# Six of sixteen probability blocks per pass turned by DMA transposes between two GpSimd copies, in an attention block on one core

## What is computed

```
q = split_heads(layernorm(x) @ Wq + bq);  k = split_heads(ctx @ Wk + bk);  v = split_heads(ctx @ Wv + bv)
scores = einsum('bhqd,bhkd->bhqk', q, k) / sqrt(32)
attn = softmax(scores, axis=-1)
out = einsum('bhqk,bhkd->bhqd', attn, v)  ->  @ Wo + bo
```

## Time and profile before

| what | value |
|---|---|
| median of 3 runs | 515.05 us (514.48 to 515.17) |
| the profiled execution | 515.1 us, its span 513.3 us, granted TensorE clock 0.998 |
| TensorE (PE) busy | 495.2 us, 96% |
| PE's weight loads | 378.2 us, 74% |
| VectorE (DVE) busy | 307.7 us, 60% |
| ScalarE (ACT) busy | 266.2 us, 52% |
| GpSimd (POOL) busy | 42.2 us, 8% |
| chain that ended last | PE 83%, ACT 7%, DVE 5%, issue 4% |

### The profile page before, as it was taken

How to read it: one execution, slowest core, us unless ns; L and a number is a source line. 1 busy time by engine, 2 the same in 40 slices (tenths; PEclk the granted TensorE clock), 3 DMA queues, 4 the chain that set the end, 5 groups by cost and what they waited for, 6 DMA issues and landing times.

```text
span 513.3 us, 9255 instructions
## 1 busy us (share of the span) xinstructions
PE 495.2 (96%) x3742; PEld 378.2 (74%) x3742; DVE 307.7 (60%) x585; ACT 266.2 (52%) x401; POOL 42.2 (8%) x34
## 2 busy tenths in 40 slices
PE   8999998999999999999999999999899998999995
PEld 6786777777777777897877778757595866877663
DVE  3757532645554553346187384579379978975962
ACT  4230037495857641328357748467345727755730
POOL 0030000000199000000000000000002010000000
PEclk9999999999999999999999999999999999999999
DMA  8900000000341022220310000298387899876001
GB/s 277 357 2 1 1 1 0 2 1 1 108 162 64 1 77 89 82 83 1 106 39 3 0 3 0 68 421 334 109 324 271 316 390 377 298 298 240 1 0 41
DMA packets 11497, 63.52 MB, mean 124 GB/s; under 512 B 1600, under 2 KB 2112, under 8 KB 4544
## 3 DMA queue, kind: packets, MB, share of 16 engines
q1 hardware_dynamic: 11168, 62.67, 32.3%
q10 hardware_dynamic: 288, 0.27, 0.2%
HBM read 62.41 MB, written 0.52 MB: 123 GB/s over the span
## 4 chain that ended last, share of the span: by engine, by line
PE 83%; ACT 7%; DVE 5%; issue 4%; POOL 0%; POOLq 0%; ACTq 0%; DVEq 0%
PE ps L1155 36%; PE ps L1225 11%; PE ps L1239 6%; PE ps L1209 5%; ACT Pm L452 4%; PE ps L1471 3%; PE ps L1473 3%; PE ps L1472 3%; PE ps L1491 3%; PE ps L1430 1%; PE ps L1431 1%; PE ps L1432 1%; PE ps L1149 1%; PE ps L1420 1%; ACT PT L460 1%
## 5 line engine op out<-in xcount | busy, mean ns | idle before, releaser
L753 DVE TENSOR_SCALAR_CACHE_REDUCE Pm<-ps,small 128x512 f32<-128x512 f32 x96 | 66.4, 748 | 30.5 <-PE ps L1209 30.3
L460 ACT COPY PT<-ps 128x512 f32<-128x512 f32 x128 | 68.5, 592 | 28.9 <-PE ps L1225 28.9
L1225 PE MATMUL ps<-ident,Pm 128*128 128x128 f32 x512 | 69.3, 277 | 3.2 <-ACT Pm L452 3.2
L1225 PEld LDWEIGHTS ps<-ident,Pm 128*128 128x128 f32 x512 | 56.5, 141 | 18.0 <-issue 11.0
L452 ACT ACTIVATE Pm<-Pm,small 128x2048 f32<-128x2048 f32 x32 | 64.3, 2011 | 3.5 <-DVE Pm L753 3.5
L733 DVE SCALAR_TENSOR_TENSOR KrL<-ps,small,KrH 128x512 fp32r<-128x512 f32 x32 | 23.9, 747 | 61.2 <-ACT KrH L438 61.2
L1155 PE MATMUL ps<-wvH,ctxH 128*128 128x512 f32 x124 | 50.3, 405 | 1.0 <-DVE V L742 1.0
L1155 PE MATMUL ps<-ctxH,wkH 128*128 128x512 f32 x124 | 51.1, 412 | 0.0
L1155 PE MATMUL ps<-ctxL,wkH 128*128 128x512 f32 x124 | 48.6, 392 | 0.0
L1155 PE MATMUL ps<-ctxH,wkL 128*128 128x512 f32 x124 | 48.5, 391 | 0.0
L1155 PE MATMUL ps<-wvH,ctxL 128*128 128x512 f32 x124 | 48.4, 390 | 0.0
(11 more groups left out here) (229 smaller groups left out, 872.3 us busy)
## 6 DMA issues: line engine op xcount, KB each, us to landing
w1raw<-in_W SPq DMA_DIRECT2D x16, 1024.0 KB, 6.1
w2raw<-in_W SPq DMA_DIRECT2D x16, 1024.0 KB, 7.3
raw<-in_ctxT SPq DMA_DIRECT2D x7, 1024.0 KB, 5.2
woF<-in_ffn_Wo SPq DMA_DIRECT2D x4, 1024.0 KB, 10.0
wo<-in_wo SPq DMA_DIRECT2D x2, 1024.0 KB, 4.9
ctx_first<-in_ctxT SPq DMA_DIRECT2D x4, 256.0 KB, 4.7
wv_raw<-in_xWv SPq DMA_DIRECT2D x2, 512.0 KB, 8.2
wq<-in_xWq SPq DMA_DIRECT2D x1, 1024.0 KB, 13.3
```

The lines of the kernel that those rows point to most:

```text
L460: act.copy(PT[:, c % 2, i, :, :].rearrange("p k t -> p (k t)"), ps[:, t_bank(p, c, i), :]).then_inc(pt_done, 1)
L753: dve.tensor_scalar(Pm[:, i, c * CH:(c + 1) * CH], ps[:, i, :], -1.0, mx[:, p % 2, i, c - 1:c] if c else NOT_YET, ALU.mult, ALU.min, accum ...
L1225: last = pe.transpose(ps[:, t_bank(p, c, i), j * P:(j + 1) * P], Pm[:, i, c * CH + j * P:c * CH + (j + 1) * P], ident[:])
```

## The change

For passes 0 to 6, chunks two and three of heads 0 to 2 are no longer turned by TensorE: six of a pass's sixteen blocks. POOL splits the 32-bit words of such a block into a plane of lower and a plane of upper halves (`stage`, 16-bit, a place for each of the two chunks), SP issues a DMA that transposes the 128 x 1024 halves into the block's own place in `Pm`, and POOL joins the halves into `PT`. A chunk's place in `stage` is written again when its DMA of the head before has landed. N(2) and N(3) now wait, head by head, for the joins (`merged`) in place of the transposes, and W(2), W(3) wait for them too. Pass 7 stays as it was.

The joins of chunk c begin when W(c - 2) has read that half of `PT`. TensorE's loop is ordered anew: W(2) goes to the next loop beside W(3), W(1) and K(3) stand together behind S(1), only T(2,3) and T(3,3) are left of chunks two and three, and 8 of the 12 matmuls of the next pass's K(0) stand before S(3) (loops 1, 2, 5 and 6; `EARLY`). The ring of keys has two places in place of three, so that ACT's eviction of K(2) waits for S(0), and DVE's stands behind N(0).

POOL no longer splits the context of batch 1: ACT makes the high halves in loop 3 (`context_high`), DVE the low ones in loops 3 and 4 (`context_low`). The loads of the context stand on SP between the transposes of pass 2.

```diff
+        def by_dma(p, c, i):
+            return p < NP - 1 and c >= PEC and i < HD
+        PEC = C // 2
+        HD = HPG - 1
...
+            def turned(p, i):
+
+                for c in range(PEC, C):
+                    sp.wait_ge(p_split, 2 * (HD * p + i) + c - PEC + 1)
+                    sp.dma_start_transpose(Pm[:, i, c * CH:(c + 1) * CH].bitcast(U16).rearrange("p (k t) -> p k t", t=T),
+                                           stage[:, c - PEC, :, :].rearrange("p h n -> p (h n)")).then_inc(p_turned[c], 16)
...
+            for p in range(G):
+                for i in range(HD):
+                    turned(p, i)
+                    if p == G - 2:
+                        context_in(i)
+                if p == G - 2:
+                    context_in(C - 1)
...
-            for c in range(C):
-
-                pool.wait_ge(raw_in[c], 32 if c else 16)
-                pool.tensor_copy(ctxH[c][:], raw[c][:]).then_inc(ctx_hi1, 1)
-                pool.wait_ge(ctx_hi1, c + 1)
-                pool.tensor_tensor(ctxL[c][:], raw[c][:], ctxH[c][:].bitcast(F32), ALU.subtract).then_inc(ctx_split1, 1)
...
+            def probs_split(p, i):
+
+                pool.wait_ge(exp_done, HPG * p + i + 1)
+                for c in range(PEC, C):
+                    if HD * p + i:
+                        pool.wait_ge(p_turned[c], 16 * (HD * p + i))
+                    words = halves_of(Pm[:, i, c * CH:(c + 1) * CH])
+                    pool.tensor_copy(stage[:, c - PEC, :, :], words.rearrange("p n h -> p h n")).then_inc(p_split, 1)
+
+            def probs_merged(p, c, i):
+
+                pool.wait_ge(p_turned[c], 16 * (HD * p + i + 1))
+                if i == 0:
+                    pool.wait_ge(pv_mm, slot_user(p, c))
+                words = halves_of(PT[:, c % 2, i, :, :].rearrange("p k t -> p (k t)"))
+                halves = Pm[:, i, c * CH:(c + 1) * CH].bitcast(U16).rearrange("p (h n) -> p h n", h=2)
+                pool.tensor_copy(words.rearrange("p n h -> p h n"), halves).then_inc(merged[c], 1)
...
                 if n >= KR:
-                    act.wait_ge(s_mm, (n if c == C - 1 else p * C) * HPG - (2 * HPG if c == C - 1 else 0))
+                    act.wait_ge(s_mm, (n - KR + 1) * HPG)
...
+                if p == G - 1:
+                    context_high(0)
+                    context_high(1)
...
-                    if p:
-                        dve.wait_ge(t_mm, n - C * HPG + 1)
+                    if p and by_dma(p - 1, c, i):
+                        dve.wait_ge(merged[c], HD * (p - 1) + i + 1)
+                    elif p:
+                        dve.wait_ge(t_mm, turned_before(p - 1, c, i) + 1)
...
                         negative_scores(p, c)
-                        if c == 1:
-                            keys(p, 3)
+                        if p == G and c == 0:
+                            context_low(3)
+                        if c < 2:
+                            keys(p, c + 2)
+                        if p == G - 1 and 0 < c < 3:
+                            context_low(c - 1)
...
+                    scores(p, 1)
+                    weighted_values(p - 1, 1)
+                    keys(p, 3)
+                    probs_T(p - 1, 2, 3)
+                    if p == G + 3:
                         masks(0)
...
+                    scores(p, 2)
+                    probs_T(p - 1, 3, 3)
+                    if early_keys(p + 1):
+                        keys(p + 1, 0, (0, EARLY))
+                    scores(p, 3)
```

More of the change, by code:

```diff
@@ L238, in perceiver_block @@
         s_mm, s_done = sem("s_mm"), sem("s_done")
+        p_split = sem("p_split")
+        merged = {c: sem(f"merged{c}") for c in range(PEC, C)}
+        p_turned = {c: sem(f"p_turned{c}") for c in range(PEC, C)}
         exp_done, t_mm = sem("exp_done"), sem("t_mm")
@@ L312, in ffn_wo_in @@
                 sp.dma_start(woF[:, k, :], a["ffn_Wo"][:, k, :]).then_inc(woF_in, 16)
+            for p in range(G, NP - 1):
+                for i in range(HD):
+                    turned(p, i)
             sp.wait_ge(k_mm, NP * C)
@@ L567, in while_values, with context_high @@
                 values(1, n // JT, n % JT)
+            def context_high(c):
+                act.wait_ge(raw_in[c], 32 if c else 16)
+                act.copy(ctxH[c][:], raw[c][:]).then_inc(ctx_hi1, 1)
             for p in range(1, NP + 1):
@@ L595, in _ @@
                             keys(p, 3)
-                        probs_T(p - 1, c, i)
+                        if not by_dma(p - 1, c, i):
+                            probs_T(p - 1, c, i)
                         if c == 3 and i == 1:
@@ L600, in _ @@
                         outputs2_T(0)
+                    if p == G - 1 and c >= 2:
+                        context_high(c)
                 if p == G:
@@ L1038, in _ @@
                 alongside(p, "keys1")
-                if p < NP:
-                    keys(p, 2)
                 for c in range(C):
@@ L1156, in product, with keys @@
                 return mm
-            def keys(p, c):
+            def keys(p, c, part=(0, 3 * KT)):
                 b, g = divmod(p, G)
@@ L1171, in keys @@
                     pe.wait_ge(s_done, p * C * HPG)
-                product(ps[:, K2_BANK if p and c == 1 else K_BANK, :], [(w[:, k, f], t[:, k, :]) for k in range(KT)
-                                           for w, t in ((wkH, ctxH[c]), (wkL, ctxH[c]), (wkH, ctxL[c]))]).then_inc(k_mm, 1)
+                pairs = [(w[:, k, f], t[:, k, :]) for k in range(KT)
+                         for w, t in ((wkH, ctxH[c]), (wkL, ctxH[c]), (wkH, ctxL[c]))]
+                for n in range(*part):
+                    mm = pe.matmul(ps[:, K2_BANK if p and c == 1 else K_BANK, :], *pairs[n], start=(n == 0),
+                                   stop=(n == len(pairs) - 1))
+                if part[1] == len(pairs):
+                    mm.then_inc(k_mm, 1)
             def values(b, c, j):
@@ L1492, in ffn_out, with early_keys @@
                 last.then_inc(f_mm, 1)
+            EARLY = 8
+            def early_keys(p):
+                return 1 < p < NP and p not in (G, G + 1)
             for p in range(1, NP + 1):
@@ L1500, in _ @@
                 if more:
-                    keys(p, 0)
+                    keys(p, 0, (EARLY if early_keys(p) else 0, 3 * KT))
                 if late:
+                    weighted_values(p - 2, C - 2)
                     weighted_values(p - 2, C - 1)
```

134 lines of the change are left out of this document (85 added, 49 removed).

## The result

The changed kernel takes 531.96 us in the median (531.57 to 532.44) against 514.76 for the kernel before beside it: a ratio of 1.0328 [1.0313, 1.0343], 17.2 us slower. The profiled execution has a span of 530.6 us (513.3 before), TensorE busy 494.4 us and 93% (495.2 and 96%), and a mean granted clock of 0.967 (0.998).

What follows compares the result with a forecast made beforehand. TensorE was taken as busy nearly throughout, so gains come from its work or waits. From 515.1 us, -3.56 + 3.95 + 0.65 - 0.5 - 1.7 - 2.25 + 0.4 = -3.0 gave 512.1 us, range 507 to 521.

Steps and rivals of the forecast that it cites:

- the steady loop: A middle loop, end of S(3) to end of S(3): 25.85 us in place of 27.62, a gain of 1.78.
- the idle time before T(0,3): TensorE's wait for ACT's last exponential in the front half of a loop: grows from 0.4 to 1.2 us.
- loops 6 and 7: Two later loops with other work on DVE: gains of 1.7 and 2.25 us.
- the prices of split (1.05) and DMA (3.2): New path in each pass: a POOL copy taken at 1.0 us, a transposing DMA at 2.7 to 3 us.
- loops 3 and 4, +3.95: Loops paying for the context's casts on ACT and subtractions on DVE: 59.2 us in place of 55.25.
- The term of loop 5, -0.5: Loop 5: front unchanged, DVE's copies and two operations stand before N(2), 1.3 us more than is idle; gain 0.5 us.
- The price of the values: Behind loop 4, W(2) and W(3) stand among the values where W(3) with a 0.35 us wait stood: +0.65 us.
- the late transposes: Rival: transposing DMAs land too late for the joins; 524 us at L = 6.5, 558 at 8.6; chance 0.16.
- L = 5.6: Landing time in us of a 256 KB transposing DMA up to which the new path costs nothing.
- POOL as the bound: Rival: at S = 2.3 POOL's twelve copies take 27.6 us a loop, about 520 us in all; chance 0.08.
- S is 1.05 and 1.42: S is the time of one POOL copy of halves in the new path, taken as 1.0 us, upper end 2.3.

Runs made afterwards that it cites:

- e8: Changed kernel with loop 3's context loads issued by ACT behind its key copies in place of SP, casts left where they were: 527.68 us.
- e1: Changed kernel with POOL's joins in loop 5 held until DVE's eight small copies are done: 527.75 us.
- e10: Changed kernel with idle matmuls at its long TensorE waits in loops 3, 4, 5 and 7, nothing else: 528.81 us.
- e9: e7 with 21 idle matmuls in TensorE's waits in loops 3, 4, 5 and 7: 510.45 us.
- e5: Changed kernel with 22 idle matmuls in TensorE's 7.50 us wait in loop 3: 528.89 us.
- e2: Changed kernel with context loads issued by ACT, casts and subtractions placed elsewhere, and the fourth cast on POOL: 522.60 us.
- e4: Changed kernel with the edits of e1 and e2 together: 518.65 us.
- e6: e4 with context loads back on SP, first behind head 0's transposes, others behind all of loop 3's; casts and last subtraction moved: 515.46 us.
- e7: e6 with POOL's joins in loop 7 held until DVE's router operations are done: 515.00 us.

## Why the prediction was wrong

The forecast of 512.1 us and its range of 507 to 521 both failed.

- **Right**: the steady loop (25.70 us against 25.85; the idle time before T(0,3) 0.90 us against 1.2), loops 6 and 7, the prices of split (1.05) and DMA (3.2), and that DVE never waits for a join in a steady loop.
- **The failed term is loops 3 and 4, +3.95.** Its casts were right: alone they cost 3.06 us (e8). What failed is the sentence that the loads are issued 7 us or more before their casts and that their place behind the transposes "is in this". The second was issued at 140.69 us, 1.4 us before the casts began, because SP's queue held it behind the transposes of head 1; TensorE waited 7.50 us, 4.4 of them for it (7.50 - 3.06). In e8 the same load is issued at K(1)'s end, and ACT does not wait for it. It also took longer, 7.6 us where the four loads of batch 1 took 4.7 to 5.2 before; the other three took 4.8 to 5.5. The 5.2 of the earlier trace rows mixes in three loads at the kernel's start; of these four it is the slowest.
- **The term of loop 5, -0.5, was mis-sized**: it took DVE's copies at the 2.31 us of the earlier trace rows. Beside POOL's joins they take 8.06, and e1 brings loop 5 back to 17.21. The 2.1 us that remain against the forecast of 15.15 are of the size of what the copies (3.09 - 2.31 = 0.8) and the two additions (1.03 + 1.66 - 2 x 0.69 = 1.3) still take more; no run takes these away. The prediction looked for POOL only as a bound on time, not as a load on DVE.
- **The sum has no term for the clock.** No row of the kernel before shows it fall in the loops. The price of the values was right to 0.1 us (76.75 in e10, 76.71 in e9, forecast 76.64) once the clock stays up; in the changed kernel it is 2.3 us more. Of the 9.3 us that loops 3 and 4 took beyond the forecast, 4.4 are the wait for the load; in e5, where the clock stayed up behind that wait and in loop 4, the two loops are 3.2 us shorter.
- **The rivals**: the late transposes, priced from L = 5.6 on, were not what happened, but e2 and e4 show that mechanism in loop 3 when the loads come from another queue (up to 8.4 us). POOL as the bound did not happen (S is 1.05 and 1.42).
- **The transposing DMA**: 256 KB land in 3.2 us in the median, against 2.0 and 2.7 us of the lone plain ones of this size in the earlier trace rows. The Trainium skill ("Advanced Engine Details and Errata", X-Bar Transpose (TRN2)) says that transposing DMAs are as fast as plain ones; this trace has them somewhat slower. The Trainium skill ("VectorE: DVE Perf Modes", The three transpose paths) gives 1309 ns for a block, by which eight blocks one after the other would be 10.5 us (an estimate from that page); the trace does not bear that out, since eight landed in 3.2.

Against the kernel before the spans differ by -1.22 (up to loop 1), -1.93, +10.04, +3.24, +2.91, +6.61, -1.44, -2.07 and +1.16 us in the order of the first table. How much of loops 3 and 4 is wait and how much is clock can't be divided exactly, since a wait that is taken away can take its fall of the clock along. Shown is that with most of the waits of loops 3, 4 and 5 mended (e6) the time is 515.46 us, and with the router held (e7) and the waits filled as well (e9) 510.45. That this lies 1.7 us under the forecast is in part luck: e9's loops 3 and 4 take 55.0 us with casts and loads placed anew, where 59.2 were forecast, and its loop 5 takes 17.6, where 15.15 were.

## What to carry to other kernels

When work is taken off the engine that is busy all the time, list what its new waits are and what the clock does behind them: here the kernel lost 17 us although TensorE had 20 us less to turn, and in the mended kernel 21 idle matmuls in waits of 0.2 to 1.2 us brought 4.5 us back. Before a load shares a queue with transfers that wait for compute, compare its issue time with the time at which an in-order engine will wait for it, and ask what stands behind that wait. An idle POOL is not free when DVE works between SBUF tiles: put its copies beside DVE's evictions from PSUM.

## What the hardware showed that was not expected

- DVE's operations between SBUF tiles slow down beside POOL's 16-bit copies: copies of 32 x 128 from 261 to 980 ns, a subtraction of 128 x 2048 from 2.29 to 2.74 and 3.16 us (3.80 in e7). N, which reads PSUM and writes SBUF, stays at 0.75. Of the router's three steps with two inputs in loop 7, two are slow beside the joins, and before none is:

```profile
343.52 0.20 DVE L1004 TENSOR_TENSOR small<-small 128x4 f32<-128x4 f32 x1
343.75 1.24 DVE L1005 TENSOR_TENSOR small<-small 128x4 f32<-128x4 f32 x1
...
345.22 1.16 DVE L1007 TENSOR_TENSOR oh<-small 128x128 f32<-128x128 f32 x1
```

```profile
325.61 0.16 DVE L927 TENSOR_TENSOR small<-small 128x4 f32<-128x4 f32 x1
325.81 0.16 DVE L928 TENSOR_TENSOR small<-small 128x4 f32<-128x4 f32 x1
...
326.20 0.29 DVE L930 TENSOR_TENSOR oh<-small 128x128 f32<-128x128 f32 x1
```

  The Trainium skill ("SBUF — State Buffer", SBUF: two separate sides) says that the two engines share one pair of ports, given to one of them for a whole instruction. By that section an operation with two SBUF inputs is among those that share; the traces agree: the two slow steps have two inputs, and the reductions with one around them kept 0.15 and 0.16. Two inputs are not needed: the small copies have one, and they slow down. The delay does not go by the operation's size: it is 0.04 to 1.5 us, for most about one POOL copy (1.0 to 1.4 us).
- The granted clock fell to 0.50 behind waits that were short and in pieces: in loop 4, 1.47 us before K(3) and 0.40 and 0.17 before S(3) were followed by a window at 0.50. The same program need not do it each time: in e5's trace loop 4 has the same waits and stays at 1.00. e6 and e7 have the same loop 3, and in their traces one fell to 0.50 behind 0.84 us of wait, the other stayed at 1.00 behind 0.58.
- Two transposes take up SP's queue for 2.6 to 3.9 us, a load of 1 MB for 0.6 (rows of SP above): what holds up a load behind them is the issue and the wait for the split. The landing counts through the split: that of head 1 waited 2.44 us for the DMA of head 0.
